# A recurrent scan with expert work between its steps: the expert work one step later, and the first gate inputs of each tile copied within SBUF

## What is computed

```python
x = x + _L0_cond_ref(x, cond, ...)     # (shared + routed) / 3, all 8 experts computed, gates mostly zero
x = x + _L1_cond_ref(x, cond, ...)

# _L1_cond_ref: inputs Xz, Xr, Xh = X @ Wx?.T + bx? for every time step, then the scan
def step(H, xs):
    xz, xr, xh = xs
    Z = sigmoid(xz + H @ Whz.T + bhz)
    R = sigmoid(xr + H @ Whr.T + bhr)
    H_tilda = tanh(xh + R * H @ Whh.T + bhh)
    H_new = Z * H + (1.0 - Z) * H_tilda
    return H_new, H_new @ Whq.T + bhq
```

## Time and profile before

| | before |
|---|---|
| median of 3 runs | 1278.68 us (1277.61 to 1278.76) |
| the profiled execution, its own time | 1277.44 us |
| its span in the trace | 1275.5 us |
| TensorE clock granted over the span | 1.00 |
| busy: PE, PEld, DVE, ACT, POOL | 98%, 70%, 78%, 63%, 1% |
| chain that ended last | PE 93%, DVE 3%, ACT 2%, issue 1%, DMA 1% |
| first and last `t_z` of the scan | 51.51 and 1269.10 us |

### The profile page before, as it was taken

The page is one execution under the profiler, slowest core; times in us unless marked ns, Lnnn a source line. Parts: engine busy times, 40 slices in busy tenths (PEclk is TensorE's granted clock), DMA queues, the critical chain, the costliest instruction groups (busy, mean ns, idle before and its releaser), DMA issues.

```text
span 1275.5 us, 84499 instructions
## 1 busy us (share of the span) xinstructions
PE 1249.8 (98%) x35704; PEld 890.8 (70%) x35704; DVE 997.2 (78%) x6111; ACT 803.3 (63%) x4402; POOL 7.4 (1%) x25
## 2 busy tenths in 40 slices
PE   9999999999999999999999999999999999999887
PEld 8877677766677776667776667776667776666554
DVE  6678888788787888878888787887877787877765
ACT  4366666666666666666666666666666666666554
POOL 1000000000000000000000000000000000000000
PEclk9999999999999999999999999999999999999999
DMA  8211011111101111011111101111011111001110
GB/s 273 57 36 43 24 38 30 42 41 34 36 24 39 38 37 45 24 37 27 44 39 35 38 21 41 35 39 45 27 33 27 44 39 33 23 21 27 33 32 11
DMA packets 76186, 51.34 MB, mean 40 GB/s; under 512 B 40609, under 2 KB 73761, under 8 KB 75809
## 3 DMA queue, kind: packets, MB, share of 16 engines
q1 hardware_dynamic: 75128, 45.29, 13.7%
q10 hardware_dynamic: 680, 0.66, 0.2%
HBM read 29.13 MB, written 16.78 MB: 36 GB/s over the span
## 4 chain that ended last, share of the span: by engine, by line
PE 93%; DVE 3%; ACT 2%; issue 1%; DMA 1%; SPq 0%
PE dn_ps L1083 27%; PE up_ps L1111 26%; PE zc_bank L1247 21%; PE r_bank L1247 14%; PE aux L1083 2%; DVE terms L1006 2%; PE dn_ps L1119 1%; ACT t_h L713 1%; PE misc L1083 1%; DVE hist L1009 1%; DMA x_all<-in_L_cond_W1e 1%; DVE t_rT L982 1%; ACT t_r L693 0%; DVE rhT L985 0%; SPq L411 0%
## 5 line engine op out<-in xcount | busy, mean ns | idle before, releaser
L982 DVE STREAM_TRANSPOSE t_rT<-t_r 128x32 f32<-128x32 f32 x1024 | 156.2, 191 | 171.1 <-ACT t_r L693 163.6
L693 ACT ACTIVATE t_r<-r_bank 128x32 f32<-128x32 f32 x1024 | 146.1, 195 | 210.2 <-PE r_bank L1247 200.2
L713 ACT ACTIVATE t_h<-zc_bank 128x32 f32<-128x32 f32 x1024 | 145.9, 195 | 207.7 <-PE zc_bank L1247 207.7
L1083 PE MATMUL dn_ps<-we_sb,x_all 128*32 128x256 f32 (+1 forms) x5144 | 274.5, 329 | 0.0
L1247 PEld LDWEIGHTS zc_bank<-whT,rhT 128*8 128x8 f32 x8192 | 118.1, 87 | 177.5 <-DVE rhT L985 176.9
L1247 PE MATMUL r_bank<-whT,hist 128*8 128x64 f32 x8192 | 210.1, 220 | 16.0 <-DVE hist L1009 13.4
L1247 PE MATMUL zc_bank<-whT,rhT 128*8 128x64 f32 x8192 | 211.0, 220 | 2.8 <-DVE rhT L985 0.3
L1247 PE MATMUL zc_bank<-whT,hist 128*8 128x64 f32 x8192 | 208.9, 219 | 0.8 <-issue 0.8
L1006 DVE STREAM_TRANSPOSE terms<-t_h 128x32 f32<-128x32 f32 x1024 | 156.5, 192 | 38.2 <-ACT t_h L713 19.7
L1247 PEld LDWEIGHTS r_bank<-whT,hist 128*8 128x8 f32 x8192 | 117.6, 88 | 94.6 <-DVE hist L1009 72.5
L1083 PEld LDWEIGHTS dn_ps<-we_sb,x_all 128*32 128x32 f32 x5144 | 137.9, 110 | 31.9 <-issue 1.0
(11 more groups left out here) (132 smaller groups left out, 1691.4 us busy)
## 6 DMA issues: line engine op xcount, KB each, us to landing
gate_inputs_by_group<-gru_raw SPq DMA_DIRECT2D x64, 192.0 KB, 2.0
gru_raw<-gate_inputs_by_group SPq DMA_DIRECT2D x256, 48.0 KB
xT_all<-in_x SPq DMA_DIRECT2D x448, 8.0 KB
x_all<-in_x SPq DMA_DIRECT2D x31, 128.0 KB
out<-gru_raw SPq DMA_DIRECT2D x31, 128.0 KB
x_all<-in_L_cond_W1e SPq DMA_DIRECT2D x4, 512.0 KB, 7.6
we_sb<-in_L_cond_W2e SPq DMA_DIRECT2D x4, 512.0 KB, 8.6
xT_all<-in_L_cond_w SPq DMA_DIRECT2D x2, 256.0 KB, 5.3
```

Source lines behind the costliest of these rows:

```text
L693: act.activation(t_r[:, i, :], r_ps[:, i * Q:(i + 1) * Q], ACT.Tanh, scale=0.5).then_inc(tr_ready, 1)
L713: act.activation(t_h[:, i, :], c_ps[:, i * Q:(i + 1) * Q], ACT.Tanh, scale=-1.0).then_inc(th_ready, 1)
L982: dve.transpose(t_rT[:, i, :], t_r[:, i, :]).then_inc(trT_done, 1)
L1083: done = pe.matmul(ps[Q * j:Q * (j + 1), col:col + cols], lhsT[:, Q * j:Q * (j + 1)], rhs, start=first, stop=last, tile_position=(0, Q * j ...
```

## The change

All places r move one step later against the scan (FIRST_STEP 7): r = 25 now falls on step 0 of an odd tile. FIRST_UPS is 30, and the second-layer piece of r = 9 and products 30 to 35 of pair 1 move from ahead of the scan into its first step. Of each tile, SP copies the inputs of steps 0, 1 and 2 straight from `xproj` to `xs` (four DMAs of 8 x 192 elements for each step), and reads only steps 3 to 15 back from memory. ACT has a semaphore for each of the three steps, and waits for `xs_first` ahead of step 3. SP's waits change places: step 8 of the tile's seeds is now waited for before the store.

```diff
+    AHEAD = 3
...
+        xs_step = [sem(f"xs_step{s}") for s in range(AHEAD)]
...
-        FIRST_STEP = 6
+        FIRST_STEP = 7
...
-        UP_ACT2_FIRST = {12: 3, 15: 4, 18: 5, 20: 6, 23: 7, 25: 8, 27: 9, 29: 10, 31: 11}
+        UP_ACT2_FIRST = {9: 2, 12: 3, 15: 4, 18: 5, 20: 6, 23: 7, 25: 8, 27: 9, 29: 10, 31: 11}
...
-        FIRST_UPS = 36
+        FIRST_UPS = 30
...
+            def step_rows(s, q):
+
+                for j in range(q * NG // PIECES, (q + 1) * NG // PIECES):
+                    sp.dma_start(xs[Q * j:Q * j + B, s, :], xproj[s::TS, j, :]).then_inc(xs_step[s], 16)
+
+            def deliver(t, q):
+
+                sp.wait_ge(xp_ready, PIECES * t + q + 1)
+                step_rows(0, q)
+                store_inputs(t, q)
+                for s in range(1, AHEAD):
+                    step_rows(s, q)
...
                     sp.wait_ge(xs_second, 16 * NG * (n + 1))
-                    for q in range(PIECES):
-                        store_inputs(n + 1, q)
                     sp.wait_ge(seeded_zc, TS * n + HALF)
                     for q in range(PIECES):
+                        deliver(n + 1, q)
+                    for q in range(PIECES):
                         sp.wait_ge(xp_stored[q], 16 * (n + 2))
-                        gate_rows(q, 0, xs_first)
+                        gate_rows(q, AHEAD, HALF, xs_first)
...
-            act.wait_ge(xs_first, 16 * NG)
+            act.wait_ge(xs_step[0], 16 * NG)
             seed_r(0, 0)
             seed_zc(0, 0)
-            consume_up(1, 2)
...
                     if after:
-                        if s + 1 == HALF:
+                        if after[1] < AHEAD:
+                            act.wait_ge(xs_step[after[1]], 16 * NG * (after[0] + 1))
+                        if after[1] == AHEAD:
+                            act.wait_ge(xs_first, 16 * NG * (n + 1))
+                        if after[1] == HALF:
                             act.wait_ge(xs_second, 16 * NG * (n + 1))
-                        if last:
-                            act.wait_ge(xs_first, 16 * NG * (n + 2))
                         seed_r(*after)
```

More of the change, by code:

```diff
@@ L474, in store_inputs, with gate_rows @@
                 sp.dma_start(by_group[groups, :, :].rearrange("j p c -> p j c"), xproj[:, groups, :]).then_inc(xp_stored[q], 16)
-            def gate_rows(q, half, done):
+            def gate_rows(q, begin, end, done):
                 for j in range(q * NG // PIECES, (q + 1) * NG // PIECES):
-                    src = by_group[j, :, :].rearrange("(b t) c -> b t c", b=B)[:, half * HALF:(half + 1) * HALF, :]
-                    sp.dma_start(xs[Q * j:Q * j + B, half * HALF:(half + 1) * HALF, :], src).then_inc(done, 16)
-            for q in range(PIECES):
-                store_inputs(0, q)
+                    src = by_group[j, :, :].rearrange("(b t) c -> b t c", b=B)[:, begin:end, :]
+                    sp.dma_start(xs[Q * j:Q * j + B, begin:end, :], src).then_inc(done, 16)
+            def step_rows(s, q):
[7 more added lines that the diff above has]
+                    step_rows(s, q)
             sp.wait_ge(xs_zeroed, 1)
             for q in range(PIECES):
+                deliver(0, q)
+            for q in range(PIECES):
                 sp.wait_ge(xp_stored[q], 16)
-                gate_rows(q, 0, xs_first)
-            sp.wait_ge(xs_first, 16 * NG)
+                gate_rows(q, AHEAD, HALF, xs_first)
             for q in range(PIECES):
-                gate_rows(q, 1, xs_second)
+                gate_rows(q, HALF, TS, xs_second)
             load_late(EARLY + 1)
```

## The result

The change is slower: **1283.69 us** in the median of 6 runs (1281.89 to 1286.7) against 1278.72 for the kernel before (6 runs beside them, 1277.61 to 1280.02), a ratio of 1.004 with a 95% interval of 1.0029 to 1.0051. The forecast was 1281.1 with a range up to 1283.0, so the result lies 0.7 us outside. In a later measurement, side by side on another occasion, the same two kernels gave 1283.77 and 1280.69, 1.0026 (1.0017 to 1.0035): the kernel before came out 2 us higher, the change as before. The profiled execution of the change took 1281.89 us, its span 1280.1.

The account below looks back on a forecast made before the run. The prediction took each step to be bound by its state-to-state chain, 2.375 us, with PE's filling just fitting beside it. Terms -1.3 + 0.05 + 1.4 + 1.0 + 1.3 = +2.4 us gave a median of 1281.1 us, range 1277.3 to 1283.0.

Parts of the forecast that it names:

- The mechanisms on ACT and DVE: Scan steps 0, 1, 2: added waits and the moved tanh lengthen steps where ACT or DVE is full; +1.4, +1.0, +1.3 us.
- A second semaphore where the states are kept: Step 0, where ACT is full: an added wait ahead of the seed costs 0.045 us, 31 times, +1.4 us (0 to 1.55).
- On DVE in places 26 and 27: Steps 1 and 2 of odd tiles, DVE full: the added wait costs 26 times 0.04, +1.0 us (0 to 1.25).
- The tanh: Router's tanh moves to step 0 of odd tiles, ahead of `t_h` on full ACT: 14 times 0.095, +1.3 us (0.7 to 1.55).
- Ahead of the scan: Before the scan's first product: PE loses work and gets there earlier, first seed at or just before PE; -1.3 us.
- the first seed is late: Scan start: a landing of 3.6 us or more leaves a gain of 0.6 or less; 1281.8 to 1282.5, chance 0.10.
- The delivery: Next tile's inputs, behind tile 0: copies and read-back arrive in time; cost 0, cover 1.1 us at the least.
- The rival of late rows at every tile: Step 0 of 31 tiles: copies landing over 4.7 us after issue make each wait; over 2.6 us from 0.08, chance 0.06.
- would miss the seed: Tile delivery: had the read-back path been kept, its last landing would come too late for the seed; no size given.
- the stalls move: Whole scan: its some 4 us of stalls may be more or fewer, 1 us either way; chance with something unseen 0.09.
- the signs named: First product 49.5, first `t_z` 50.2; step 0 2.52 odd, 2.42 even; L1006 1.22 in odd tiles' steps 1, 2; others 2.375.

Follow-up runs that it names:

- The idle waits: Kernel before plus an ACT wait on a long-reached semaphore ahead of the seeds of steps 0, 1, 2: 1281.83 against 1280.29 us, 1.0018.
- the free waits: Changed kernel with the router's tanh behind `seed_zc` and input waits on the second half of the previous step's `t_r`: 1283.03 against 1280.29 us, 1.0025.
- the tanh behind the seed: Changed kernel with the router's tanh moved from ahead of `t_h` to behind `seed_zc`: 1283.92 us against 1280.29 for the kernel before, 1.0038.
- the second trace: Profiled execution of the unedited change measured again: 1283.77 us in 9 runs against 1280.69 for the kernel before, 1.0026; its tile 0 took 39.76 us.
- the kernel with the better order of tile 0: Changed kernel, tanh behind `seed_zc`, waits on `t_r`'s second half; tile 0's copies in step order, ACT issuing its two stores: 1281.69 us, 1.0013 against kernel before.
- the spare copies: Kernel before plus twelve unused copies a tile into a spare SBUF buffer, no added ACT wait: 1280.64 against 1280.69 us, 1.0002.
- the kernel with the shift alone: Places one step later and FIRST_UPS 30, all steps still delivered by store and read-back: 1292.83 us in 2 runs, 1.0096 against the kernel before.
- with 8 products: Both kernels with 8 small PE products of zeros ahead of the experts' first unit: change 1284.49 us, kernel before 1280.63; each otherwise unedited.
- with 64: Both kernels with 64 small PE products of zeros ahead of the experts' first unit: change 1306.52 us, kernel before 1305.74 (1306.67 the second time).
- the copies with free waits and no shift: The change's copies with places r as before, input waits on the second half of `t_r`: 1281.11 us against 1280.69 for the kernel before, 1.0007.

## Why the prediction was wrong

**The mechanisms on ACT and DVE were right, their sizes nearly.** A second semaphore where the states are kept: forecast 31 x 0.045 = 1.4, measured 31 x 0.035 = 1.1. On DVE in places 26 and 27: forecast 1.0, measured 28 x 0.035 = 1.0. The tanh: forecast 14 x 0.095 = 1.3, measured 14 x 0.10 = 1.4. (The estimate from the page "ScalarE: Activation LUTs" of the Trainium skill, section "What ACT_TABLE_LOAD costs", 0.106 us, is as good.) Together 3.5 against 3.7. The idle waits and the free waits show the first two by adding and by removing them, in the steps and in the totals; the tanh behind the seed shows the third in the steps alone.

**The step that failed is "Ahead of the scan": "I take the copy near the store ... and the term at -1.3 us, its bounds -1.36 and -0.6".** It measured -0.28 before the first `t_z` and +0.32 in the step behind it (2.74 us against 2.42), 0.0 in all, and in the second trace another +1.1 in the step after that: 0.0 to +1.1, outside its bounds. The doubt was laid on the landing of step 0's copies, and that was good: the seed started 1.7 us after the last issue began (48.55 to 50.25), 2.1 in the kernel with the better order of tile 0. (The section of the Trainium skill that the forecast names, "Anatomy of one DMA" on the page "DMA: Bandwidth & Descriptors", is about DMAs that GpSimd issues, and these are SP's; its 2.0 us happens to be near.) What was wrong stands in the sentence before it, "two copies (0.3 us each, as the two reads that take 0.60)". The issue of a copy was not in the trace, the nearest row was taken for it without bounds, and its measured duration is 0.56 to 0.60. Seven DMAs ahead of step 0's last two copies, six of them copies at twice the price, moved the last one from 46.35 to about 48.5, and those of steps 1 and 2, whose places behind it the forecast had not costed in tile 0 at all, to 52. The kernel with tile 0's order shows the cause: with step 0's copies issued first, the scan's first product came 5.13 us after the same start, as forecast, where the kernel before has 6.41 and the change 6.2 (50.53 after 44.31). The rival "the first seed is late" named the place; it blamed the landing, though it did name the small DMAs ahead in SP's queue, and it allowed 1281.8 to 1282.5. With the measured term the forecast would have been 1282.4 to 1283.5.

**The delivery was right.** Zero cost with its cover: no seed behind tile 0 waited. SP needs 7.2 us for a tile's copies instead of the 4 of the forecast, which its waiting in each tile also covers; the spare copies show this by themselves. The rival of late rows at every tile didn't come (its 0.08 us at 31 tiles is 2.5 us, not over 2.6, which changes nothing), but the sentence that the read-back path "would miss the seed" did, in the kernel with the shift alone (18 tiles, 12.3 us).

**The rest is as large as the scatter.** Priced by measurement, the change costs 3.5 us and 0.0 to 1.1 at the start, 3.5 to 4.6. Four pairs of kernels give 5.0, 3.1, 3.9 (with 8 products) and 0.8 (with 64, 4 runs each). The first lies 0.4 over the upper price. In the profiled executions some 1.4 us of the difference are such long steps (3.9 against 2.4), and both executions lie below their medians, by 1.3 us before and 1.8 after; no trace shows what the median executions have. The rival "the stalls move" had the right size, 1 us, but had its chance as a case by itself, when it comes on top of every case. The range's upper end names a late seed and a stall together, yet 1283.0 leaves only 0.5 us above the late seed's 1282.5; with the whole 1 us it would still have missed by 0.2. With the start as measured and 1 us of stalls on top the range would have reached 1284.5. That the result lies outside by 0.7 us and not inside is therefore in part chance; that the start's term was wrong is not. Of the signs named, those for steps 0, 1 and 2 came as said (2.51 for 2.52, 2.41 for 2.42, L1021 at 1.22), those for the first product (50.53 for 49.5) and the first `t_z` (51.23 for 50.2) did not.

None of the versions that use the copies beats the kernel before. The nearest, the copies with free waits and no shift, can't be told from it.

## What to carry to other kernels

On a chain that is full at one place per tile, a wait is an operation: put on an instruction that has no other wait it cost nothing here (2.38 us a step), on one that has, 0.035 to 0.055 us each time. Before a transfer's landing is argued about, count what its queue needs to issue it, and give an issue of a shape that isn't in the trace bounds of its own. And where two kernels are 0.3% apart, compare several pairs of them: steps that are long in one execution and not in the next make 2 to 9 us here, and one profile of a kernel can lie at either end.

## What the runs showed of the hardware

**Issuing a small copy is dearer than issuing a large store.** SP's own time, in the change: the copy (6 KB), the store (192 KB) and the read-back.

```profile
L487 SPq DMA_DIRECT2D gru_raw<-gru_raw x384: 563/564/1758, 43.7 to 1234.8; - x192
```
```profile
L476 SPq DMA_DIRECT2D gate_inputs_by_group<-gru_raw x64: 381/441/452, 45.0 to 1232.5; - x64
```
```profile
L482 SPq DMA_DIRECT2D gru_raw<-gate_inputs_by_group x256: 263/297/1837, 52.1 to 1238.9; - x128
```

The size doesn't decide it; that source and target both lie in SBUF may, which was not tried by itself.

**With 64 small products of zeros in a row the clock fell.** PE's products of zeros in the kernel before with 64 of them, and with 8; the trace has two records for each:

```profile
6.58 25.16 PE L1293 MATMUL aux<-zeros 128*128 128x8 f32 x128
```
```profile
6.24 1.85 PE L1293 MATMUL aux<-zeros 128*128 128x8 f32 x16
```

And windows of the two kernels:

```profile
8.00:10.00 2.00, 2.00 (x15) 2.00 (x15) 1.54 (x3) 1.15 (x2) 0.00 (x0) 0.73 0.99 249
10.00:12.00 2.00, 2.00 (x11) 2.00 (x11) 0.15 (x1) 0.00 (x0) 0.00 (x0) 0.50 1.04 296
...
32.00:36.00 4.00, 4.00 (x21) 4.00 (x20) 0.84 (x2) 0.38 (x1) 0.00 (x0) 0.50 0.70 141
36.00:40.00 4.00, 4.00 (x35) 3.99 (x34) 2.73 (x7) 2.57 (x6) 0.00 (x0) 0.97 0.21 44
```
```profile
14.00:40.00 26.00, 26.00 (x259) 24.49 (x258) 19.92 (x57) 11.92 (x24) 6.31 (x9) 1.00 0.85 245
```

The third number from the end, ahead of the DMA share, is the granted clock. With 8 it stays at 1.00. With 64 it falls while the products run, between 8 and 10 us, and stays at the lower of its two levels, 0.50 or 1.2 GHz, until 36 us; the experts' first product starts at 31.59. The 8 products took 1.85 us, 0.23 us each, all at 1.00; the 64 took 25.16, 0.39 each. By the former 64 would take some 15 us (an estimate), so the lower clock makes about 10 of the 25. The first `t_z` is at 76.64 instead of 51.64: nearly all of the 25 us are the products themselves. (The 0.15 us a product in one of the expectations comes of a part of the row alone, 9.59 us with 55 of the 128 records.)
